# An attention kernel in which VectorE's step is reordered: the first head's maximum, the reading of outputs, the second head's maximum

## The chip, the cores and the metric
The kernel runs on one core of a Trainium2 chip. The metric is the device time of one execution in microseconds (us). Its engines work side by side and meet only at semaphores: TensorE (PE, with its weight loads as PEld), VectorE (DVE), ScalarE (ACT), GpSimd (POOL) and SyncE (SP), which issues the DMAs here.

## The reference
The input x is 2 sequences of 2048 tokens and 1024 features. A block of causal attention with 16 heads of 64 features, and then a gated low-rank layer:

```python
q = (x @ wq.T + bq).reshape(B, S, H, hd)      # k, v alike; x is the layer norm of the input
scores = jnp.einsum('bqhd,bkhd->bhqk', q, k) * inv_sqrt_hd
scores = jnp.where(causal[None, None, :, :], -jnp.inf, scores)
probs = jax.nn.softmax(scores, axis=-1)
attn = jnp.einsum('bhqk,bkhd->bqhd', probs, v).reshape(B, S, D)
return attn @ wo.T + bo
...
x = x + _layernorm(attention(_layernorm(x)))
x = x + _layernorm(ffn(_layernorm(x)))        # 8 experts, gates, the best one's low-rank update
```

## The kernel before
**Stages.** The norm of the first sequence and the first projections take some 110 us. Then come 16 pairs of heads (p = 0 to 15, eight for each sequence), about 110 us each, up to 1945 us: this is `attend_phase`. Then `finish_phase` does the output projection and the gated layer, tile by tile; the change doesn't touch it. Values of f32 are split into two f16 halves, high and low, and a product is made of three matmuls. In pairs 0 to 6 the norm of the second sequence's x runs between the other work (`norm_tiles`), in pairs 6 and 7 its transposes (`TURN_STEPS`), and in pair 15 the output weights are prepared (`center_wo`, `wo_high`, `wo_low`).

**A pair.** Its 16 rows of 128 queries are gone through in eight rounds, each of a long row (t of 8 to 15) and a short one (t of 0 to 7). A round is two steps, one round three, so a pair has NSTEP = 17 steps; a step holds eight blocks of 128 keys for each of two heads, in one or two parts. Most pairs open rounds at steps 0, 2, 4, 6, 9, 11, 13 and 15; pairs 0 and 15 take the rows upwards and open at 0, 2, 4, 6, 8, 10, 12 and 14. A part whose last block lies on the diagonal needs the causal mask in that block. Scores run LAG = 3 steps ahead of the product with v. A task is one step of one head; numbers n count tasks.

**Each engine's order is written out by hand**, one `body(p, kind)` per engine, with waits on semaphore counts. What step i of pair p does:
- TensorE (body from L613): `scores` of step i + 3 for both heads (L524), which waits until the exponential of the first head, one step before, has freed a buffer of the ring of three (`exp_done`); a unit or half a unit of the next pair's q, k or v projection (`project`, L593 to L599; `UNIT_AT` has the plan), which waits until the unit before it has been read (`full_done`); then `times_v` of step i for both heads (L547 to L549). In a step that opens a round the first head's `times_v` waits for `part_done` and `short_done`, since it overwrites the outputs of the last round.
- VectorE (body from L795): if the step opens a round, `output_read` (L746, L748, L752) and `output_sum` (L761, L764) of the last round and `row_min` (L737); then `row_max` of step i + 3 (masks L716, maxima L723, biases L728); then the low half of a weight (`split_weight`, L681 to L685), the reading of a finished unit (`unit_full`, L696, L701) and pieces of the norm.
- ScalarE (body from L946): for each head the exponentials (L894) and the high half of the probabilities (L901). Between the two heads stand `chunk_factors` (L909, which need `row_min` and the reading), once or twice a pair the high half of finished rows (`rows_high`, L919) and the high half of a unit (`unit_high`, L884).
- GpSimd (body from L1079): `long_rows` (L1062), which needs `output_sum`, the low half of the probabilities (`probs_low`, L1049) of the first head, `rows_low` (L1070), `unit_low` (L1054), and `probs_low` of the second head.
- SyncE: the DMA transposes of the probabilities (pt, L413), each after `probs_low`; finished rows are stored (L420) two steps after `rows_low`.

The lines that make VectorE's opening step before:

```python
if evacuate:
    output_read(*done)
    output_sum(*done)
if opens:
    row_min(p, r)
step = step_of(p, i, kind)
if step:
    row_max(*step)
```

Of the kernel before, what the change touches and what calls it, by code (L numbers as in the profile page):

```python
# [7 lines left out]
ALU = mybir.AluOpType  # L8
# [3 lines left out]
AX_X = mybir.AxisListType.X  # L12
# [176 lines left out]
def attend_phase(nc, x, w_pairs, mask_in, xn_scratch, o_scratch, arena, fin):  # L189
    with ExitStack() as ctx:  # L190
# [161 lines left out]
        def half_done(p):  # L352

            return first_step(p, N_ROUND // 2)
# [282 lines left out]
        def _(dve):  # L637
# [63 lines left out]
                    nc.vector.tensor_scalar(full[u % 2][:], bank, PROJ_UNSCALE,  # L701
                                            bias_cols[:, WHICH[m]:WHICH[m] + 1], ALU.mult, ALU.add).then_inc(full_done, 1)

            def row_max(p, i):
                step, n = steps_of(p)[i], NTASK * p + 2 * i
                dve.wait_ge(s_done, n + 2)
                places = []
                for part in step.parts:
                    first = places[-1][2] if places else 0
                    places.append((part, first, first + part[2] * P))  # L710
                masked = 2 * (QT * p + sum(is_diagonal(part) for step in steps_of(p)[:i] for part in step.parts))
                for h in range(2):
                    for part, first, end in places:
                        if is_diagonal(part):
                            last = s_ps[(n + h) % S_RING][:, end - P:end]
                            nc.vector.tensor_tensor(last, last, mask[:], ALU.add).then_inc(mask_done, 1)  # L716
                found = 2 * parts_before(p, i)
                for h in range(2):
                    for (t, k0, nb, acc), first, end in places:
                        if is_diagonal((t, k0, nb, acc)):  # L720
                            masked += 1
                            dve.wait_ge(mask_done, masked)
                        nc.vector.tensor_reduce(neg_max[:, step.round, acc, h:h + 1], s_ps[(n + h) % S_RING][:, first:end],  # L723
                                                AX_X, ALU.max, negate=True).then_inc(max_done, 1)
                    for (t, k0, nb, acc), first, end in places:
                        found += 1
                        dve.wait_ge(max_done, found)
                        nc.vector.tensor_scalar(exp_bias[:, step.round, acc, h:h + 1], neg_max[:, step.round, acc, h:h + 1],  # L728
                                                SOFTMAX_SCALE, LOG_P_SCALE, ALU.mult, ALU.add).then_inc(bias_done, 1)

            def row_min(p, r):

# [63 lines left out]
            def body(p, kind):  # L796
                for i in range(NSTEP):
                    r, opens = steps_of(p)[i].round, steps_of(p)[i].opens
                    done = (p, r - 1) if i else (p - 1, N_ROUND - 1)
                    evacuate = opens and done[0] >= 0  # L800
                    if evacuate:
                        output_read(*done)
                        output_sum(*done)
                    if opens:
                        row_min(p, r)
                    step = step_of(p, i, kind)
                    if step:
                        row_max(*step)
                    split = next_split(p, i - 1)
                    if split:  # L810
                        split_weight(*split)
                    for u in units_ending(kind, i):
                        unit_full(units_of(p), u)
                    for tile in norm_tiles(p, i, 0):
                        norm_stats(LN_TILES + tile, x_in[:], x_loaded[X_RING], tile)
                    for tile in norm_tiles(p, i, 1):
                        norm_apply(LN_TILES + tile, x_in[:])
                    for tile in norm_tiles(p, i, 2):
                        xn_low(LN_TILES + tile, x_in[:], xn)
                    if kind == "last":  # L820
                        if i == 6:
                            dve.wait_ge(unit_done, N_UNIT * PAIRS)
                            nc.vector.memset(fin["mix_w2"][:], 0.0).then_inc(mix_set, 1)
                            nc.vector.memset(fin["bias"][:], 0.0).then_inc(mix_set, 1)
                        if 3 <= i < 3 + WO_BY_ACT:
                            center_wo(i - 3)
                        if i in (7, 8, 9, 11):
                            center_wo({7: 4, 8: 5, 9: 6, 11: 7}[i])
                        for n, row in enumerate(("bo_row", "degen", "bias")):
                            if i == 12 + n:  # L830
                                center_rows(n, fin[row][:])
                        if 13 <= i < 13 + KT - WO_LOW_EARLY:
                            wo_low(WO_LOW_EARLY + i - 13)
                        if i == 16:
                            split_ffn_weights()
                if kind == "last":
                    output_read(p, N_ROUND - 1)
                    output_sum(p, N_ROUND - 1)
# [15 lines left out]
                unit_full(0, u)  # L854
            dve.wait_ge(consts_loaded, 32)
            for i in range(LAG):
                row_max(0, i)
                unit_full(0, LAST_CHUNK + i)
                if i == 1:
                    split_weight(1, "k")  # L860
# [3 lines left out]
        def _(act):  # L864
# [81 lines left out]
            def body(p, kind):  # L946
                for i in range(NSTEP):
                    step = step_of(p, i, kind)
                    if step:
                        exponentials(*step, 0)  # L950
                    if steps_of(p)[i].opens:
                        chunk_factors(p, steps_of(p)[i].round)
                    if i == half_done(p) or i == 0 and p > 0:
                        rows_high(2 * p + (0 if i else -1))
                    for u in units_ending(kind, i - 1):
                        unit_high(units_of(p), u)
                    if step:
                        exponentials(*step, 1)
                    if i == NSTEP - 1:
                        for u in units_ending(kind, i):  # L960
                            unit_high(units_of(p), u)
                    split = next_split(p, i)
                    if split:
                        split_weight(*split)
                    if kind == "last" and 2 <= i < 2 + WO_BY_ACT:
                        wo_sum(i - 2)
                    if kind == "last" and 6 <= i < 6 + KT:
                        wo_high(i - 6)
                    for n, row in enumerate(("bo_row", "degen", "bias")):
                        if kind == "last" and i == 11 + n:  # L970
                            row_sum(n, fin[row][:])
                    if kind == "last" and i == 15:
                        for n in range(4):
                            ffn_high(n)
                    for tile in norm_tiles(p, i, 1):
                        if tile > 0:
                            act.wait_ge(xn_stored, 16 * tile)
                        xn_high(LN_TILES + tile, x_in[:], xn)
                if kind == "last":
                    rows_high(2 * p + 1)  # L980
# [46 lines left out]
        def _(pool):  # L1027
# [50 lines left out]
            def body(p, kind):  # L1078
                for i in range(NSTEP):  # L1079
                    step = step_of(p, i, kind)  # L1080
                    if steps_of(p)[i].opens and (p or i):
                        long_rows(*((p, steps_of(p)[i].round - 1) if i else (p - 1, N_ROUND - 1)))
                    if step:
                        probs_low(*step, 0)
                    if i == half_done(p) or i == 0 and p > 0:
                        rows_low(2 * p + (0 if i else -1))
                    for u in units_ending(kind, i - 1):
                        unit_low(units_of(p), u)
                    if step:
                        probs_low(*step, 1)  # L1090
                    if i == NSTEP - 1:
                        for u in units_ending(kind, i):
                            unit_low(units_of(p), u)
                    for tile in norm_tiles(p, i, 0):
                        norm_scale(LN_TILES + tile)
                    if kind == "last" and 6 <= i < 6 + WO_LOW_EARLY:
                        wo_low(i - 6)
                if kind == "last":
                    long_rows(p, N_ROUND - 1)
                    rows_low(2 * p + 1)  # L1100
# [704 lines left out]
```

## Time and profile before

| | us |
|---|---|
| runs | 2399.49, 2399.89 (median), 2405.32 |
| profiled execution, its own time | 2399.97 |
| its span, first to last instruction | 2397.7 |
| TensorE busy | 2274.8 |
| VectorE, ScalarE, GpSimd busy | 1677.1, 1740.6, 1632.0 |
| TensorE's mean granted clock | 0.979 of full speed |

The profile is of one execution. In it an engine's time is busy, or idle with a releaser: the instruction or DMA whose semaphore ended the wait. Line numbers (L716) are those of the kernel before. Idle time under 0.15 us is not listed as a wait. An instruction may start a little before its forerunner on the same engine has ended, since they are pipelined; matmuls overlap more strongly.

### The profile page before, as it was taken

What the parts mean: (1) busy time and instruction counts of PE and PEld (TensorE: products, weight loads), DVE (VectorE), ACT (ScalarE), POOL (GpSimd) and SP (SyncE); (2) the same over time, 40 slices, a digit from 0 to 9 for tenths busy, and PEclk for the clock granted to TensorE, in tenths of its full rate; (3) what the DMA queues carried; (4) which work ended last, traced back from release to release, by engine and by line L of the source; (5) the groups of instructions that cost most, each with busy time, mean ns of one, the idle gap of its engine ahead of it and who ended that gap; (6) DMA issues with size and microseconds to landing.
All of it is one profiled execution on the core that took longest, in us unless ns stands there. A gap on an engine that the chain in (4) does not pass through costs nothing. (4 is left out here: it accounts for less than half of the span.)

```text
span 2397.7 us, 70688 instructions
## 1 busy us (share of the span) xinstructions
PE 2274.8 (95%) x28666; PEld 1450.1 (60%) x28666; DVE 1677.1 (70%) x4148; ACT 1740.6 (73%) x2380; POOL 1632.0 (68%) x1291
## 2 busy tenths in 40 slices
PE   6999999999999998899999999999999679999996
PEld 4566667575757666557575757575766445445453
DVE  8587777767777766566666666666676846777777
ACT  6577777777777766677777777777787846666665
POOL 3588888888878876778888888888898822222221
PEclk9999999999999999999999999999999789999997
DMA  9699999999999999999999999999999986656662
GB/s 246 129 196 200 197 212 203 198 193 203 213 196 202 200 202 199 206 198 194 176 197 179 190 181 182 190 183 186 181 191 198 235 166 152 170 152 171 151 166 80
DMA packets 1380627, 447.43 MB, mean 187 GB/s; under 512 B 1325104, under 2 KB 1358272, under 8 KB 1380304
## 3 DMA queue, kind: packets, MB, share of 16 engines
q1 hardware_dynamic: 1380304, 442.91, 99.4%
q8 instruction: 228, 3.74, 0.6%
q14 instruction: 95, 0.78, 0.1%
HBM read 67.95 MB, written 41.94 MB: 46 GB/s over the span
## 5 line engine op out<-in xcount | busy, mean ns | idle before, releaser
L1049 POOL TENSOR_TENSOR hl<-probs,hl 128x1024 f16<-128x1024 f32 x544 | 1166.3, 2150 | 347.6 <-ACT hl L901 345.6
L894 ACT ACTIVATE probs<-s_ps,exp_bias 128x1024 f32<-128x1024 f32 (+7 forms) x768 | 632.7, 853 | 324.4 <-DVE exp_bias L728 319.6
L723 DVE TENSOR_REDUCE neg_max<-s_ps 128x1 f32<-128x1024 f32 (+7 forms) x768 | 675.7, 904 | 166.9 <-PE s_ps L524 166.8
L901 ACT ACTIVATE hl<-probs 128x1024 f16<-128x1024 f32 x544 | 575.0, 1057 | 82.9 <-DMA pt<-hl 66.9
L547 PE MATMUL o_ps<-v,pt 128*128 128x65 f16 x4352 | 434.4, 194 | 48.7 <-DMA pt<-hl 40.7
L547 PEld LDWEIGHTS o_ps<-v,pt 128*128 128x128 f16 x4352 | 402.2, 97 | 78.5 <-DMA pt<-hl 36.4
L548 PE MATMUL o_ps<-v,pt 128*128 128x65 f16 x4352 | 434.7, 195 | 0.0
L549 PE MATMUL o_ps<-v,pt 128*128 128x65 f16 x4352 | 433.5, 193 | 0.0
L524 PE MATMUL s_ps<-nat 64*128 64x512 f16 (+3 forms) x3840 | 409.4, 351 | 22.2 <-ACT probs L894 18.8
L548 PEld LDWEIGHTS o_ps<-v,pt 128*128 128x128 f16 x4352 | 401.6, 97 | 19.2
L549 PEld LDWEIGHTS o_ps<-v,pt 128*128 128x128 f16 x4352 | 402.1, 98 | 0.0
L597 PE MATMUL u_ps<-arena,w 128*128 128x512 f16 x1000 | 380.8, 381 | 4.8 <-DVE full L696 2.8
L598 PE MATMUL u_ps<-arena,w 128*128 128x512 f16 x1000 | 379.0, 379 | 0.0
L599 PE MATMUL u_ps<-arena,w 128*128 128x512 f16 x1000 | 379.0, 379 | 0.0
L593 PE MATMUL u_ps<-w,arena 128*128 128x128 f16 x2016 | 346.1, 220 | 3.5 <-DVE arena L673 3.1
L594 PE MATMUL u_ps<-w,arena 128*128 128x128 f16 x2016 | 345.1, 220 | 0.0
L595 PE MATMUL u_ps<-w,arena 128*128 128x128 f16 x2016 | 344.9, 220 | 0.0
L524 PEld LDWEIGHTS s_ps<-nat 64*128 64x128 f16 x3840 | 164.0, 95 | 159.6 <-issue 32.3
L593 PEld LDWEIGHTS u_ps<-w,arena 128*128 128x128 f16 x2016 | 197.9, 98 | 45.0 <-issue 40.5
L701 DVE TENSOR_SCALAR full<-u_ps,bias_cols 128x512 f32<-128x512 f32 x125 | 93.8, 751 | 153.9 <-PE u_ps L599 153.6
L594 PEld LDWEIGHTS u_ps<-w,arena 128*128 128x128 f16 x2016 | 198.2, 98 | 0.1
L595 PEld LDWEIGHTS u_ps<-w,arena 128*128 128x128 f16 x2016 | 198.2, 98 | 0.0
(185 smaller groups left out, 3578.3 us busy)
## 6 DMA issues: line engine op xcount, KB each, us to landing
w_raw<-in_w_pairs SPq DMA_DIRECT2D x48, 576.0 KB, 4.8
o_scratch<-o_hl SPq DMA_DIRECT2D x64, 256.0 KB, 3.2
out<-result SPq DMA_DIRECT2D x31, 512.0 KB, 3.0
x_in<-in_x SPq DMA_DIRECT2D x27, 512.0 KB, 5.1
pt<-hl SPq DMA_TRANSPOSE x544, 5.3
xn_scratch<-xn SPq DMA_DIRECT2D x16, 512.0 KB, 4.8
xn<-in_x SPq DMA_DIRECT2D x11, 512.0 KB, 3.9
x_in_c<-in_x SPq DMA_DIRECT2D x10, 512.0 KB, 4.0
```

The costliest lines, as they stand in the source:

```text
L524: mm = nc.tensor.matmul(s_ps[(n + h) % S_RING][:, at:end], qk[HEADS[h], q, rows], qk[HEADS[h], k, keys], start=(q == q_lo), stop=(q == q_h ...
L547: nc.tensor.matmul(dst, lo, v_hi, start=first, stop=False)
L548: nc.tensor.matmul(dst, hi, v_lo, start=False, stop=False)
L549: mm = nc.tensor.matmul(dst, hi, v_hi, start=False, stop=last)
L593: nc.tensor.matmul(dst, xt[:, 1, k, toks], hi[:, k, :], start=first, stop=False)
L594: nc.tensor.matmul(dst, xt[:, 0, k, toks], lo[:, k, :], start=False, stop=False)
L595: mm = nc.tensor.matmul(dst, xt[:, 0, k, toks], hi[:, k, :], start=False, stop=last)
L597: nc.tensor.matmul(bank, lo[:, k, :], xt[:, 0, k, toks], start=first, stop=False)
L723: nc.vector.tensor_reduce(neg_max[:, step.round, acc, h:h + 1], s_ps[(n + h) % S_RING][:, first:end], AX_X, ALU.max, negate=True).then_inc ...
L894: last = nc.scalar.activation(probs_of(n)[:, cols], s_ps[n % S_RING][:, cols], ACT.Exp, bias=exp_bias[:, step.round, acc, h:h + 1], scale= ...
L901: nc.scalar.activation(hl_of(n, 0), probs_of(n), ACT.Copy).then_inc(p_hi_done, 1)
L1049: nc.gpsimd.tensor_tensor(hl_of(n, 1), probs_of(n), hl_of(n, 0), ALU.subtract).then_inc(p_lo_done, 1)
```

## The change
VectorE's `row_max` now does one head per call. In a step it does the first head (masks, maxima, biases), then `output_read`, `row_min`, the second head, and `output_sum` last. So in every step the second head's masks come after the first head's biases, and in an opening step the reading comes after the first head. ScalarE does `rows_high` after the second head's exponentials instead of before `unit_high`. GpSimd does `long_rows` after the first head's `probs_low` and `unit_low`, and `rows_low` after the second head's `probs_low`. TensorE, SyncE, all tiles and all instructions stay as they are.

```diff
@@ VectorE
-            def row_max(p, i):
+            def row_max(p, i, h):
                 step, n = steps_of(p)[i], NTASK * p + 2 * i
                 dve.wait_ge(s_done, n + 2)
...
-                masked = 2 * (QT * p + sum(is_diagonal(part) for step in steps_of(p)[:i] for part in step.parts))
-                for h in range(2):
-                    for part, first, end in places:
-                        if is_diagonal(part):
-                            last = s_ps[(n + h) % S_RING][:, end - P:end]
-                            nc.vector.tensor_tensor(last, last, mask[:], ALU.add).then_inc(mask_done, 1)
-                found = 2 * parts_before(p, i)
-                for h in range(2):
-                    for (t, k0, nb, acc), first, end in places:
...
+                diagonals = sum(is_diagonal(part) for part in step.parts)
+                masked = 2 * (QT * p + sum(is_diagonal(part) for step in steps_of(p)[:i] for part in step.parts)) + h * diagonals
+                found = 2 * parts_before(p, i) + h * len(step.parts)
+                for part, first, end in places:
+                    if is_diagonal(part):
+                        last = s_ps[(n + h) % S_RING][:, end - P:end]
+                        nc.vector.tensor_tensor(last, last, mask[:], ALU.add).then_inc(mask_done, 1)
+                for (t, k0, nb, acc), first, end in places:
...
                     evacuate = opens and done[0] >= 0
+                    step = step_of(p, i, kind)
+                    if step:
+                        row_max(*step, 0)
                     if evacuate:
                         output_read(*done)
-                        output_sum(*done)
                     if opens:
                         row_min(p, r)
-                    step = step_of(p, i, kind)
                     if step:
-                        row_max(*step)
+                        row_max(*step, 1)
+                    if evacuate:
+                        output_sum(*done)
@@ ScalarE
-                    if i == half_done(p) or i == 0 and p > 0:
-                        rows_high(2 * p + (0 if i else -1))
                     for u in units_ending(kind, i - 1):
                         unit_high(units_of(p), u)
                     if step:
                         exponentials(*step, 1)
+                    if i == half_done(p) or i == 0 and p > 0:
+                        rows_high(2 * p + (0 if i else -1))
@@ GpSimd
+                    if step:
+                        probs_low(*step, 0)
+                    for u in units_ending(kind, i - 1):
+                        unit_low(units_of(p), u)
                     if steps_of(p)[i].opens and (p or i):
                         long_rows(*((p, steps_of(p)[i].round - 1) if i else (p - 1, N_ROUND - 1)))
                     if step:
-                        probs_low(*step, 0)
+                        probs_low(*step, 1)
                     if i == half_done(p) or i == 0 and p > 0:
                         rows_low(2 * p + (0 if i else -1))
-                    for u in units_ending(kind, i - 1):
-                        unit_low(units_of(p), u)
-                    if step:
-                        probs_low(*step, 1)
```

## Rows read from the trace of the kernel before

**Rows 1.** The page, part 1: busy us of each engine, share of span, instructions.

```profile
PE 2274.8 (95%) x28666; PEld 1450.1 (60%) x28666; DVE 1677.1 (70%) x4148; ACT 1740.6 (73%) x2380; POOL 1632.0 (68%) x1291
```

**Rows 2.** Waits of TensorE, whole span: total us, times, longest us.

```profile
PE o_ps L547 <- DMA pt<-hl: 40.7, 31, 3.2
PE s_ps L524 <- ACT probs L894: 18.8, 23, 2.5
...
PE o_ps L547 <- DVE o_rows L752: 6.4, 3, 3.1
```

**Rows 3.** Stretches: length, busy us of five engines, granted clock, DMA share, GB/s.

```profile
480.00:540.00 60.00, 56.84 (x942) 43.06 (x942) 41.09 (x96) 44.70 (x58) 48.24 (x30) 0.97 1.18 193
600.00:660.00 60.00, 57.90 (x977) 44.54 (x974) 43.37 (x110) 44.88 (x59) 50.09 (x33) 1.00 1.16 215
...
1080.00:1740.00 660.00, 659.73 (x9596) 444.00 (x9592) 445.31 (x1137) 512.80 (x674) 538.26 (x328) 1.00 1.07 186
```

**Rows 4.** Waits of TensorE, 170 to 1860 us.

```profile
PE s_ps L524 <- ACT probs L894: 12.7, 16, 2.5
```

**Rows 5.** Waits of TensorE, 1860 to 1945 us.

```profile
PE o_ps L547 <- DMA pt<-hl: 19.9, 17, 2.9
```

**Rows 6.** Timeline of VectorE, pair 10, step 9: start us, us, instruction, idle before.

```profile
1340.91 0.43 DVE L746 TENSOR_TENSOR o_part<-o_ps,factor 128x260 f32<-128x260 f32 x1 [0.76 <-PE o_ps L549]
...
1341.45 0.29 DVE L752 TENSOR_TENSOR o_rows<-o_ps,inv_short 128x128 f32<-128x128 f32 x1
1341.66 0.41 DVE L761 TENSOR_REDUCE o_long<-o_part 128x130 f32<-128x260 f32 x1
...
1342.19 0.16 DVE L737 TENSOR_REDUCE bias_min<-exp_bias 128x2 f32<-128x4 f32 x1
1342.33 0.89 DVE L716 TENSOR_TENSOR s_ps<-s_ps,mask 128x128 f32<-128x128 f32 x4
1343.13 1.27 DVE L723 TENSOR_REDUCE neg_max<-s_ps 128x1 f32<-128x384 f32 x2
1344.32 0.27 DVE L728 TENSOR_SCALAR exp_bias<-neg_max 128x1 f32<-128x1 f32 x2
```

**Rows 7.** Timeline of TensorE, pair 10, steps 2, 4 and 9.

```profile
1294.02 1.48 PE L524 MATMUL s_ps<-nat 64*128 64x512 f16 x18
...
1300.62 0.19 PE L547 MATMUL o_ps<-v,pt 128*128 128x65 f16 x1
...
1307.72 1.47 PE L524 MATMUL s_ps<-nat 64*128 64x512 f16 x12
...
1311.72 0.19 PE L547 MATMUL o_ps<-v,pt 128*128 128x65 f16 x1
...
1340.81 1.48 PE L524 MATMUL s_ps<-nat 64*128 64x384 f16 x18
...
1344.91 0.19 PE L547 MATMUL o_ps<-v,pt 128*128 128x65 f16 x1
```

**Rows 8.** Timeline of both engines, pair 15, step 8.

```profile
1885.57 0.29 DVE L752 TENSOR_TENSOR o_rows<-o_ps,inv_short 128x128 f32<-128x128 f32 x1
...
1886.01 0.19 PE L547 MATMUL o_ps<-v,pt 128*128 128x65 f16 x1 [2.12 <-DVE o_rows L752]
```

**Rows 9.** Timeline of VectorE and TensorE, pair 4 into pair 5.

```profile
675.00 3.15 DVE L667 SCALAR_TENSOR_TENSOR xn<-x_in,xn 128x1024 f16<-128x1024 f32 x1
678.07 1.21 DVE L723 TENSOR_REDUCE neg_max<-s_ps 128x1 f32<-128x1024 f32 x1
...
680.76 0.39 PE L524 MATMUL s_ps<-nat 64*128 64x512 f16 x2 [0.95 <-ACT probs L894]
```

**Rows 10.** Timeline of VectorE, ScalarE and TensorE, pair 4, steps 9 and 10.

```profile
629.69 0.41 DVE L746 TENSOR_TENSOR o_part<-o_ps,factor 128x260 f32<-128x260 f32 x1
...
633.32 1.26 ACT L894 ACTIVATE probs<-s_ps,exp_bias 128x384 f32<-128x384 f32 x2 [5.36 <-DVE exp_bias L728]
...
634.73 0.39 PE L524 MATMUL s_ps<-nat 64*128 64x512 f16 x2 [0.63 <-ACT probs L894]
```

More of the change, by code:

```diff
@@ L717, in row_max @@
-                found = 2 * parts_before(p, i)
-                for h in range(2):
-                    for (t, k0, nb, acc), first, end in places:
[L720 to L729, printed above, removed]
+                diagonals = sum(is_diagonal(part) for part in step.parts)
@@ new lines, in row_max @@
+                masked = 2 * (QT * p + sum(is_diagonal(part) for step in steps_of(p)[:i] for part in step.parts)) + h * diagonals
[5 more added lines that the diff above has]
+                for (t, k0, nb, acc), first, end in places:
+                    if is_diagonal((t, k0, nb, acc)):
+                        masked += 1
+                        dve.wait_ge(mask_done, masked)
+                    nc.vector.tensor_reduce(neg_max[:, step.round, acc, h:h + 1], s_ps[(n + h) % S_RING][:, first:end],
+                                            AX_X, ALU.max, negate=True).then_inc(max_done, 1)
@@ L731, in row_min @@
+                for (t, k0, nb, acc), first, end in places:
+                    found += 1
+                    dve.wait_ge(max_done, found)
+                    nc.vector.tensor_scalar(exp_bias[:, step.round, acc, h:h + 1], neg_max[:, step.round, acc, h:h + 1],
+                                            SOFTMAX_SCALE, LOG_P_SCALE, ALU.mult, ALU.add).then_inc(bias_done, 1)
             def row_min(p, r):
@@ L856, in _ @@
             for i in range(LAG):
-                row_max(0, i)
+                for h in range(2):
+                    row_max(0, i, h)
                 unit_full(0, LAST_CHUNK + i)
```

## The prediction

> **What bounds the kernel now.** I read the busy shares first. TensorE is busy for 95% of the span and no other engine for more than 73% [rows 1], so the first question is what TensorE waits for. Its waits answer that [rows 2]: 40.7 us for transposed probabilities (pt) to land, 18.8 us for an exponential that frees a score buffer, and 6.4 us, in three places, for VectorE's reading of outputs. Then I asked where these lie. From 1080 to 1740 us, pairs 8 to 13 of the 16, TensorE is busy 659.73 of 660 us at full clock, the other three engines under 82% [rows 3]. There the schedule hides everything beside TensorE: a new order on the other engines can gain nothing in these six pairs, it can only uncover something. What can be gained lies in pairs 0 to 7 and in the last pair: of the waits for an exponential, 12.7 us in 16 places lie between 170 and 1860 us [rows 4]. The last pair (1860 to 1945 us) has 19.9 us of waits for pt [rows 5].
>
> **The step that the change touches.** A pair has 17 steps, eight of which open a round. In an opening step TensorE issues the scores of three steps ahead, then a piece of projection, then times_v, whose first matmul must wait until VectorE has read the last round's outputs. Times from the scores' end (S), in pair 10, step 9: the scores run from 1340.81 to 1342.29, times_v starts at 1344.91, which is S + 2.62 [rows 7]. VectorE reads from 1340.91 to 1341.74, sums, takes the minimum and starts the masks at 1342.33, 0.04 us after S [rows 6]. So today reading, sum and minimum (1.42 us from 1340.91 to 1342.33) fit under the 1.48 us of scores and cost nothing. The maxima aren't held up by them either. This is the profile's point against the change: the first head's maximum can't start before S whatever the order is, and the reading loses its cover.
>
> **VectorE's new step, priced from the same rows.** First head: masks at S + 0.04, two instead of four. Four masks put the maximum 0.80 later, so 0.20 each [rows 6]; with two the maximum starts at about S + 0.43. Maxima and biases of one head take 1.46 (1343.13 to the end of the biases at 1344.59) and end at S + 1.90. The next instruction starts about 0.08 before its forerunner's end (o_long at 1341.66, o_rows ends at 1341.74), so the reading starts at S + 1.82 and ends 0.83 later at S + 2.65. From VectorE's end to TensorE's first matmul is 0.15 (1885.86 to 1886.01) [rows 8]. So times_v may start at S + 2.80.
>
> It is due at S + 2.62 after half a v unit, at S + 2.53 after half a q or k unit (1309.19 to 1311.72), and at S + 5.1 after a whole unit (1295.50 to 1300.62) [rows 7]. Whole units hide the reading; half units miss it by 0.18 or 0.27. With one diagonal block (one mask) the reading ends 0.11 earlier, miss 0.16; with none it is in time. Pairs 1 to 5 and 8 to 13 have the half-unit openings 4, 9, 13 and 15 (0.16 + 0.18 + 0.18 + 0.27 = 0.79 us a pair). Over pairs 0 to 14 there are 18 of 0.27, 29 of 0.18 and 9 of 0.16: 11.5 us. Some 1.2 us of it fall in pair 7 and late in pair 14, where TensorE waits for pt anyway: **10.3 us**. The unknown is the fit of a few tenths: 0.15 less at each of 56 places is 8 us less, 0.1 more is 6 us more.
>
> **What comes behind it in the step.** Reading, minimum, the second head (masks at S + 2.7, biases done at S + 4.6), then sum and reciprocal end at about S + 5.1, where the second head's bias ended at S + 3.7 before. In openings 4 and 13 a unit's result is read after that (0.7 us) and TensorE wants its bank at the next projection, due at about S + 5.6: it misses by about 0.1. GpSimd's finished row (0.4 us) now waits behind the first head's subtraction (2.13 us) and a unit, and in opening 9 ScalarE's copy of finished rows, now last, waits for it before the next step's first exponential: 0.05 to 0.1. Together 0.3 us in each of 11 pairs: **3 us**.
> VectorE is 1.4 us later at the end of an on-time opening step. Where it then has splits or norm work and no idle time before the next maximum, and ScalarE and TensorE have no slack either, TensorE pays that. Pair 4, step 15 is the pattern: xn for 3.15 us to 678.15, the maximum at 678.07, and TensorE 0.95 us late at 680.76 [rows 9]. Five openings are like this (pair 0 step 2, pair 1 steps 6 and 15, pairs 4 and 5 step 15), with 0.7 to 1.4 us left after the slack of each: **5 us**. Elsewhere ScalarE and TensorE have more slack than the delay.
>
> **What it gives.** The first head's exponential starts 0.4 us earlier where VectorE was on time with two diagonals, but pairs 8 to 13 have no wait for it. It gains where VectorE was late. Pair 4, step 9: reading at 629.69 instead of 628.5, ScalarE idle 5.36 us until 633.32, TensorE 0.63 late at 634.73 [rows 10]. Masks first would start that exponential 1.4 us earlier; this stall and the next one, of 0.46 at 640.90, go. With smaller ones: **minus 1.6 us**. In step 4 of pairs 1 and 5 VectorE is late too: stalls of 1.70 and 1.16 us for the exponential go, but the reading, put behind the maximum, makes times_v wait 1.65 and 1.11: nothing.
> In the last pair the openings 6 to 12 have no projection and times_v would wait up to 7.5 us in all for the reading (four times S + 2.8 against its start now). But the second head's pt mostly lands later anyway [rows 5], and its stalls take the delay: **1 us**, with bounds 0 and 7.5. The row copies that move on GpSimd and ScalarE cost nothing more there: both heads' subtractions now precede them. That moves transposes earlier, up to 4 us of the 19.9 if TensorE gets them sooner.
> SyncE's queue doesn't change in order; the stores of rows are issued two steps after the copy, so 3 us of delay are covered.
>
> **Sum:** 10.3 + 3 + 5 - 1.6 + 1 = 17.7 us on the span of 2397.7 [rows 1, 3] gives 2415.4. The profiled execution took 2399.97 us, 2.3 more than its span and 0.1 above the median of the runs shown, so the forecast is **2418 us**.
>
> **The rivals.**
> *Hidden after all* (2396 to 2407): the new waits are 0.16 to 0.27 us each and rest on handoffs read from a late place [rows 8]. If they are 0.15 shorter and the slack behind takes the rest, about 5 us stay: 2405. For it: all margins are small. Against: four independent rows put the reading behind S + 2.53.
> *Faster* (2387): in pairs 0 to 7 and the last, where VectorE or ScalarE are late, the earlier first head takes away the waits for exponentials. All 12.7 us of [rows 4] gone and nothing else uncovered gives 2385.0 and 2387. It decides from the point where more of these stalls hang on VectorE's order than on ScalarE's own load. For it: pair 4, step 9. Against: most of the others follow a split, a norm copy or a row copy on ScalarE, which the change moves by less than a step.
> *VectorE's backlog* (2436): norm work and splits in pairs 0 to 6 push the maxima over more steps than the five counted. Twice the 5 us, the last pair's 7.5 in full and the upper end of the 56 waits (6 more) give 18 us more.
> *The clock* (2445): stalls of up to 1.2 us left the granted clock at 1.00 from 600 to 660 us; in the window from 480 to 540 us with one wait of 3.2 us it was 0.97, which is 1.8 us lost [rows 3, 2]. If the new short waits brought one such drop in each of 15 pairs, 27 us would come on top of the forecast. The Trainium skill, "TensorE: Matmul & The Clock Gate", "A second HAM failure mode: psum-queue depth-cycling", has a kernel whose frequent tiny idles between groups of matmuls made the clock swing and cost throughput; by that rule the clock would be this rival, and the trace of before doesn't bear it out for waits this short.
>
> **How the numbers follow.** Forecast 0.50 (its own range 2407 to 2430), hidden 0.24, faster 0.14, backlog 0.08, clock 0.04. The range for 8 in 10 reaches from 2394, which leaves out most of the faster case, to 2438, which takes in half of the backlog case; the clock is left out. Faster and slower begin 0.3% from before, 7.2 us, about what a measurement of this kernel can tell from no change: above 2407.1 lie the forecast, the backlog and the clock, 0.62; within lies 0.24; below 2392.7 lies 0.14.
>
> **What would show it.** In the profile after, TensorE's waits should have a new entry for o_rows in pairs 8 to 13, some 24 waits of 0.1 to 0.3 us (those under 0.15 us are not listed, but TensorE's busy time from 1080 to 1740 us falls below 659.7), at half-unit openings alone. VectorE should idle up to S in opening steps instead of before the reading. The wait for the exponential at step 10 of pair 4 should be gone and the one at the turn into pair 5 be longer. If TensorE has no new waits in pairs 8 to 13, the handoff is mis-sized; if the waits for pt in pair 7 or the last pair shrink by over 5 us, the transposes were not the limit there.

## The result and the profile after

| | before | after |
|---|---|---|
| median of the runs, us | 2400.76 | 2440.76 |
| lowest and highest | 2399.49, 2405.32 | 2435.84, 2444.03 |
| ratio, 95% interval | | 1.0159 [1.0146, 1.0172] |
| profiled execution: its own time, span | 2399.97, 2397.7 | 2441.16, 2439.0 |

The change makes the kernel 40 us slower. The forecast was 2418 us with a range up to 2438: the sign was right, the size less than half of it.

The page, part 1, and the waits of TensorE over the whole span (us in total, times, longest), of after:

```profile
PE 2285.1 (94%) x28666; PEld 1448.3 (59%) x28666; DVE 1725.1 (71%) x4148; ACT 1746.8 (72%) x2380; POOL 1659.1 (68%) x1291
...
PE s_ps L524 <- ACT probs L897: 40.8, 32, 2.7
PE o_ps L547 <- DMA pt<-hl: 28.5, 26, 3.3
PE o_ps L547 <- DVE o_rows L751: 17.6, 11, 4.8
```

Against [rows 1, 2] VectorE is busy for 48 us more and GpSimd for 27 us more, although both execute the same instructions as often. That is the first thing to see: some instructions have become longer. TensorE's waits for the exponential have grown from 18.8 to 40.8 us; those for the reading from 6.4 to 17.6, most of it in the last pair, where those for pt fell.

The stretches of [rows 3] that are comparable (length, busy us of PE, PEld, DVE, ACT, POOL, granted clock, DMA share, GB/s), and TensorE's waits from 1110 to 1770 us, of after:

```profile
1080.00:1740.00 660.00, 645.88 (x9261) 430.33 (x9257) 453.19 (x1095) 502.14 (x658) 533.44 (x318) 1.00 1.04 181
...
PE s_ps L524 <- ACT probs L897: 9.7, 11, 1.3
PE o_ps L547 <- DVE o_rows L751: 0.6, 2, 0.4
```

In this stretch TensorE is idle for 14.1 us where it was idle for 0.3 in [rows 3], at a clock of 1.00. The listed waits are mainly for exponentials, up to 1.3 us long, and the forecast has no such term there.

Since TensorE's order is the same in both kernels, its step ends can be subtracted one by one (after minus before, from the two traces). In pairs 9, 10, 11 and 13, the ordinary pairs of what follows, the difference is 3.1 us each (in pair 12 it is 3.5, with 0.44 at step 14):

| step | us a pair | what TensorE waits for |
|---|---|---|
| 4, 9, 13, 15 | 0.18, 0.21, 0.21, 0.30 | the reading of outputs, as forecast (0.16, 0.18, 0.18, 0.27) |
| 5, 14, 11 | 0.02, 0.08, 0.10 | the unit's result, and the rows on ScalarE (forecast 0.3 together) |
| 8 | 0.59 | exponential, not forecast |
| 0 of the next pair | 1.40 | exponential, not forecast |

The forecast's terms for such a pair were 0.79 and 0.3, and 1.11 was measured. The other 2.0 us are new. Over all pairs the turns (step 0 of pairs 2 to 14) make 21.3 us and step 8 (pairs 1 to 14) 7.8 us of the span's 41.3.

**What happens before the turn.** Timeline of VectorE, then of GpSimd, then of TensorE, after, from pair 10, step 15 into pair 11 (start us, us, instruction, idle before):

```profile
1416.65 1.57 DVE L681 TENSOR_SCALAR bv_row<-w_raw 128x128 f32<-128x128 f32 x1
1418.14 2.19 DVE L685 SCALAR_TENSOR_TENSOR w<-w_raw,w 128x1024 f16<-128x1024 f32 x1
1420.26 1.21 DVE L722 TENSOR_REDUCE neg_max<-s_ps 128x1 f32<-128x1024 f32 x1
...
1416.01 2.13 POOL L1052 TENSOR_TENSOR hl<-probs,hl 128x1024 f16<-128x1024 f32 x1 [3.54 <-ACT hl L904]
1418.10 1.15 POOL L1057 TENSOR_TENSOR nat<-full,nat 128x512 f16<-128x512 f32 x1
1419.22 1.37 POOL L1065 TENSOR_TENSOR o_rows<-o_long,inv_long 128x128 f32<-128x128 f32 x1
...
1422.95 1.26 PE L524 MATMUL s_ps<-nat 64*128 64x512 f16 x14 [1.32 <-ACT probs L897]
```

The same place before, VectorE and then GpSimd:

```profile
1385.03 0.22 DVE L681 TENSOR_SCALAR bv_row<-w_raw 128x128 f32<-128x128 f32 x1
1385.16 1.22 DVE L685 SCALAR_TENSOR_TENSOR w<-w_raw,w 128x1024 f16<-128x1024 f32 x1
1387.01 1.23 DVE L723 TENSOR_REDUCE neg_max<-s_ps 128x1 f32<-128x1024 f32 x1 [0.63 <-PE s_ps L524]
...
1382.37 0.39 POOL L1062 TENSOR_TENSOR o_rows<-o_long,inv_long 128x128 f32<-128x128 f32 x1
1386.19 2.17 POOL L1049 TENSOR_TENSOR hl<-probs,hl 128x1024 f16<-128x1024 f32 x1 [3.43 <-ACT hl L901]
```

Before, the bias row took 0.22 us and the weight split 1.22, with GpSimd idle until 1386.19, and 0.63 us were left before the next maximum. After, the bias row starts at 1416.65, while GpSimd's subtraction runs, and ends at 1418.22, just after that ends (1418.14). The split then stands against GpSimd's unit, which ends at 1419.25, and ends at 1420.33: 1.08 us later, nearly its own 1.22. And GpSimd's row product, 0.39 us when alone, starts at 1419.22 and ends at 1420.59, when the split is over. They don't slow each other in proportion: whichever comes second stands still until the first has ended. Bias row and split end 2.3 us later than their own lengths ask for (1416.65 + 1.35 = 1418.00). The next maximum starts 2.8 us after the end of its scores (1417.49) instead of at once, its exponential is late too, and TensorE starts the scores 1.32 us late.

The other place is the split of k's weight in step 6, timeline of VectorE and GpSimd, after:

```profile
1356.03 2.84 DVE L685 SCALAR_TENSOR_TENSOR w<-w_raw,w 128x1024 f16<-128x1024 f32 x1
...
1355.65 2.13 POOL L1052 TENSOR_TENSOR hl<-probs,hl 128x1024 f16<-128x1024 f32 x1 [2.48 <-ACT hl L904]
1357.74 2.14 POOL L1057 TENSOR_TENSOR nat<-full,nat 128x512 f16<-128x512 f32 x1
```

The split again ends (1358.87) 1.09 us after the subtraction (1357.78). Two steps on, at 1362.09, TensorE waits 0.52 us for an exponential.

**How often.** By line, min/median/max in ns; first before (L681, L685), then after (L681, L685):

```profile
L681 DVE TENSOR_SCALAR bv_row<-w_raw x16: 216/218/227, 13.6 to 1725.0; 128x128 f32<-128x128 f32 x16
L685 DVE SCALAR_TENSOR_TENSOR w<-w_raw,w x48: 1212/1216/2344, 13.7 to 1752.4; 128x1024 f16<-128x1024 f32 x48
```

```profile
L681 DVE TENSOR_SCALAR bv_row<-w_raw x16: 217/1575/1633, 13.4 to 1766.2; 128x128 f32<-128x128 f32 x16
L685 DVE SCALAR_TENSOR_TENSOR w<-w_raw,w x48: 1212/2190/2839, 13.6 to 1794.0; 128x1024 f16<-128x1024 f32 x48
```

The two meet because of when each starts. VectorE reaches the bias row at S + 5.0 where it was S + 3.6, and GpSimd's first subtraction of the step starts at about S + 4.4 (S + 4.8 before). Before, the split was through, or had at least begun; now the subtraction gets in first. The Trainium skill, "SBUF — State Buffer", "Who interferes with whom", states this rule: an instruction of VectorE with two inputs in SBUF, or a tensor_scalar in a 2-port mode, and a GpSimd instruction that reads SBUF exclude each other for a whole instruction, and the order of issue decides who blocks. The rows agree in both directions. The split has two inputs in SBUF; the bias row is a tensor_scalar with one, and that it ran in a 2-port mode no run shows by itself, only that it was held up like the split.

### The profile page after: what moved, and what is told of

It is laid out like the page before. It is cut to its first block and busy times, and to the rows that moved or that the text cites. A ratio compares the mean times of both kernels' runs of the same rounds, so it can differ in the third digit from the quotient of the medians.

```text
span 2439.0 us, 70688 instructions
## 1 busy us (share of the span) xinstructions
PE 2285.1 (94%) x28666; PEld 1448.3 (59%) x28666; DVE 1725.1 (71%) x4148; ACT 1746.8 (72%) x2380; POOL 1659.1 (68%) x1291
## 5 line engine op out<-in xcount | busy, mean ns | idle before, releaser
L524 PE MATMUL s_ps<-nat 64*128 64x512 f16 (+3 forms) x3840 | 410.2, 352 | 45.0 <-ACT probs L897 40.8
L717 DVE TENSOR_TENSOR s_ps<-s_ps,mask 128x128 f32<-128x128 f32 x512 | 128.7, 291 | 214.6 <-PE s_ps L524 214.3
L593 PEld LDWEIGHTS u_ps<-w,arena 128*128 128x128 f16 x2016 | 197.4, 98 | 45.0 <-issue 40.6
L597 PEld LDWEIGHTS u_ps<-arena,w 128*128 128x128 f16 x1000 | 97.8, 98 | 169.9 <-issue 69.3
L594 PEld LDWEIGHTS u_ps<-w,arena 128*128 128x128 f16 x2016 | 197.7, 98 | 0.1
```

What stands on the lines that cost most here:

```text
L524: mm = nc.tensor.matmul(s_ps[(n + h) % S_RING][:, at:end], qk[HEADS[h], q, rows], qk[HEADS[h], k, keys], start=(q == q_lo), stop=(q == q_h ...
L593: nc.tensor.matmul(dst, xt[:, 1, k, toks], hi[:, k, :], start=first, stop=False)
L594: nc.tensor.matmul(dst, xt[:, 0, k, toks], lo[:, k, :], start=False, stop=False)
L597: nc.tensor.matmul(bank, lo[:, k, :], xt[:, 0, k, toks], start=first, stop=False)
```

## The experiments

Ten kernels, all compared with the kernel before on the same chip (there 2400.89, 2401.99 and 2405.76 us in the three groups of runs). "As before" and "as after" name the order of one engine's instructions in an opening step. The cuts of code that show an order are shortened: conditions and arguments are partly left out. "Less than after" compares the two medians; the kernels before beside them differ by 1.2 us at most.

**1. VectorE's change alone.** VectorE as after; ScalarE and GpSimd as before:

```diff
 # ScalarE, GpSimd: the bodies of the kernel before
 # VectorE:
+row_max(*step, 0); output_read(*done); row_min(p, r)
+row_max(*step, 1); output_sum(*done)
```

> The change on VectorE alone; ScalarE and GpSimd keep the order of before. Theory (the loss is VectorE's: the reading behind the first head's maximum, and a weight split that runs while GpSimd subtracts): nearly the whole loss stays, 2430 to 2440 us, TensorE busy from 1080 to 1740 us stays near 646 us. Rival (the loss comes from finished rows on GpSimd and ScalarE being late): 2400 to 2412 us and busy over 656 us.

Measured 2414.48 us, ratio 1.0056 [1.0036, 1.0075]: 13.6 us of the 40, so the expectation was wrong. The ordinary pair loses 1.5 us: the same waits for the reading, 0.49 at step 11, nothing at the turn, nothing at step 8. The timeline (VectorE, GpSimd, pair 10, step 15) says why:

```profile
1395.36 0.21 DVE L681 TENSOR_SCALAR bv_row<-w_raw 128x128 f32<-128x128 f32 x1
1395.48 1.22 DVE L685 SCALAR_TENSOR_TENSOR w<-w_raw,w 128x1024 f16<-128x1024 f32 x1
...
1395.52 1.43 POOL L1065 TENSOR_TENSOR o_rows<-o_long,inv_long 128x128 f32<-128x128 f32 x1 [4.24 <-DVE inv_long L763]
```

VectorE is as late as in after. But GpSimd starts its step with the row product, which waits for the inverse that VectorE writes just ahead of the split. So the split is always first and GpSimd stands still (1.43 us instead of 0.39), which costs TensorE nothing.

**2. The rows alone.** VectorE as before; ScalarE and GpSimd as after (the second and third parts of the change's diff).

> The change on ScalarE and GpSimd alone; VectorE keeps the order of before. Theory: 2398 to 2405 us, no new wait of TensorE in pairs 8 to 13. Rival (rows late are the loss): over 2420 us.

Measured 2406.59, ratio 1.0027 [1.0017, 1.0037], a little above the range expected, and the expectation of no new wait in pairs 8 to 13 was wrong: it loses 0.70 us at step 11 of each of them and nothing else in an ordinary pair. ScalarE, pair 10:

```profile
1360.17 1.06 ACT L919 ACTIVATE o_hl<-o_rows 128x1024 f16<-128x1024 f32 x1 [0.59 <-POOL o_rows L1062]
1361.14 1.10 ACT L894 ACTIVATE probs<-s_ps,exp_bias 128x1024 f32<-128x1024 f32 x1
```

GpSimd's row is late, ScalarE's copy waits 0.59 us for it, and the next step's exponential stands behind. Together the parts cost 13.6 + 5.7 = 19 us. The whole costs 40: half of the loss is an interaction. That 19 us is near the 17.7 forecast for the whole is in part luck: the 0.49 and 0.70 us at step 11 were forecast as 0.1 at most.

**3. The reading put first again.** After, with VectorE's reading ahead of the first head (then minimum, second head, sum):

```diff
-row_max(*step, 0); output_read(*done)
+output_read(*done); row_max(*step, 0)
```

> The kernel after, with the reading of outputs put back ahead of the first head's maximum; row_min, the second head and the sum stay as changed. Theory: the half-unit openings lose their 0.2 to 0.3 us waits (1.1 us a pair), but the split after the sum stays late by about 0.8 us instead of 1.4 and still meets GpSimd's subtraction: 2405 to 2420 us. Rival (the reading's place is the whole loss): within 4 us of before, 2397 to 2405 us.

Measured 2404.56, ratio 1.0013 [1.0001, 1.0025], which fits the range of the rival and lies just below that of the theory. All waits for the reading in pairs 8 to 13 are gone and 0.31 us at step 11 are left. VectorE, GpSimd, pair 10, step 15:

```profile
1386.23 0.21 DVE L681 TENSOR_SCALAR bv_row<-w_raw 128x128 f32<-128x128 f32 x1
1386.35 1.22 DVE L685 SCALAR_TENSOR_TENSOR w<-w_raw,w 128x1024 f16<-128x1024 f32 x1
...
1386.35 3.21 POOL L1052 TENSOR_TENSOR hl<-probs,hl 128x1024 f16<-128x1024 f32 x1 [3.47 <-ACT hl L904]
```

The bias row now starts at S + 4.3, only 0.12 us before the subtraction. VectorE keeps its 0.21 and 1.22 us, and it is GpSimd that takes 3.21 us instead of 2.13: the theory had the meeting right and who would stand still wrong. Moving the reading by one place brings back both the four short waits and the order of the two engines; by itself this run can't say which of them is worth what.

**4. Two splits one step earlier.** After, with the splits of k and v moved ahead by one step:

```diff
-SPLITS = {"mid": {2: "q", 5: "k", 14: "v"}, ...
+SPLITS = {"mid": {2: "q", 4: "k", 13: "v"}, ...
```

> The kernel after, with the k and v weight splits of ordinary pairs moved by a step, so that VectorE's part follows steps 5 and 14, which open no round, instead of 6 and 15. Theory: the stalls of 1.4 us at the turn of the pair and 0.6 us at step 8 vanish in 11 pairs: about 20 us faster than after, 2412 to 2424 us, with the 1.1 us a pair of late readings left. Rival (the turn's stall is the reading's delay alone): no change from after, 2436 to 2444 us.

Measured 2449.09, ratio 1.0200 [1.0182, 1.0219]: a miss of 25 us. The stalls at the turn and at step 8 are gone in pairs 8 to 13 (0.00 against before), but a new one of 1.7 to 7.6 us stands at step 6 of 11 pairs, 43 us in all. ScalarE waits for the DMA of the raw weights 88.0 us in all, against 20.8 in after: with two steps instead of three between the splits of q and k, k's weight is asked for before it has been loaded, and VectorE waits behind ScalarE. So the experiment removed the suspected cost and added another one.

```profile
ACT w L877 <- DMA w_raw<-in_w_pairs: 88.0, 16, 9.9
...
DVE bias_cols L683 <- ACT w L877: 60.0, 15, 7.2
```

**5. Only v's split one step earlier.**

```diff
-SPLITS = {"mid": {2: "q", 5: "k", 14: "v"}, ...
+SPLITS = {"mid": {2: "q", 5: "k", 13: "v"}, ...
```

> The changed kernel with one weight split of an ordinary pair moved one step ahead, that of v from behind step 15 (an opening step) to behind step 14. Theory (this split at this place is what makes the turn into the next pair late): the turn's stall, 1.32 us at step 0 of the next pair, goes in the 11 pairs concerned, the 0.5 us at step 8 stay, as do the waits for the outputs: 13 to 16 us faster than the changed kernel, 2424 to 2429. Rival (the turn is late by the sum and the reading, which stand behind the first head's maximum, and not by the split): 2436 to 2442.

Measured 2417.59, ratio 1.0065 [1.0050, 1.0080]: 23 us less than after. The 1.40 us at the turn are gone in each of pairs 9 to 13, the 3.3 and 3.9 us at the turns into pairs 5 and 6 as well, and the 0.59 us at step 8 remain. Over all pairs the turns give 20.7 us back. It was better than expected because I had counted 11 turns at 1.4 and not the two larger ones; some 2.5 us more are a start of pair 0 that came earlier in this trace.

**6. GpSimd as before**, VectorE and ScalarE as after:

```diff
+if steps_of(p)[i].opens and (p or i): long_rows(...)
 if step: probs_low(*step, 0)
+if i == half_done(p) or i == 0 and p > 0: rows_low(...)
 for u in units_ending(kind, i - 1): unit_low(units_of(p), u)
-if steps_of(p)[i].opens and (p or i): long_rows(...)
 if step: probs_low(*step, 1)
-if i == half_done(p) or i == 0 and p > 0: rows_low(...)
```

> VectorE and ScalarE in the order of the changed kernel, GpSimd in the order of the kernel before. Theory (VectorE's weight split is held up by GpSimd's subtraction, 2.13 us long, which in the changed kernel starts just ahead of it): here GpSimd begins an opening step with the rows' product, which waits for the inverse that VectorE writes right ahead of the split, so the split starts first and keeps its 1.2 us; the stalls at the turn (1.4 us) and at step 8 (0.6 us) of each pair are gone, and what is left is VectorE's order alone (2414) and up to 0.7 us in each of 11 pairs at step 11 (8 us): 2414 to 2425, with TensorE busy near 651 to 654 us between 1080 and 1740. Rival (the opening steps are late because ScalarE's rows come last, GpSimd's order is of no account): 2433 to 2442, as the changed kernel.

Measured 2408.85, ratio 1.0029 [1.0018, 1.0040], 5 us below the range expected. VectorE's lateness is untouched (the bias row starts at S + 5.0), and 32 us of the loss are gone with the order of one other engine. VectorE, GpSimd, pair 10, step 15:

```profile
1389.59 0.21 DVE L681 TENSOR_SCALAR bv_row<-w_raw 128x128 f32<-128x128 f32 x1
1389.71 1.21 DVE L685 SCALAR_TENSOR_TENSOR w<-w_raw,w 128x1024 f16<-128x1024 f32 x1
...
1389.75 1.43 POOL L1065 TENSOR_TENSOR o_rows<-o_long,inv_long 128x128 f32<-128x128 f32 x1 [4.25 <-DVE inv_long L763]
```

Step 11 gains 0.11 us where experiment 1 lost 0.49 and up to 0.7 was expected: with the row product early, ScalarE's copy is better off last.

**7. The same lateness without a second operand in SBUF.** After, with the split's two instructions on VectorE replaced, from the weights of pair 2 on, by sums of the same lengths that read one operand. The low halves of the weights and the biases are left out from there on.

```diff
+if p >= 2:
+    nc.vector.tensor_reduce(split_to[:, 0:1], w_raw[:, KT * P:W_COLS], AX_X, ALU.add)
+    nc.vector.tensor_reduce(split_to[:, 1:2], w_raw[:, 0:KT * P], AX_X, ALU.add).then_inc(w_lo_done, 1)
+    return
```

> The changed kernel, but from the third pair on VectorE's two instructions of a weight split (the bias and the low half) are sums over a row of the same lengths that read one operand in SBUF and write one number; the low halves of the weights and the biases are not computed for those pairs. Theory (the split is slow because VectorE and GpSimd then share the way to SBUF, and the split with two operands there is the one that must wait): it takes about 1.2 us again wherever it stands, the stall at the turn goes and that at step 8 too, about 2.0 us in each of some 10 pairs: 2415 to 2424. If only the writing or any reading in SBUF is enough to be held up, it stays at 2433 to 2442. Rival (the split comes 1.3 us later than before, and that lateness alone makes the next scores' maximum late): 2433 to 2442 as well, but with the split at 1.2 us in the trace.

Measured 2411.74, ratio 1.0042 [1.0027, 1.0057], 29 us less than after and 3 below the range expected. Every order, GpSimd's included, is that of after. VectorE, GpSimd, pair 10, step 15:

```profile
1396.06 0.27 DVE L682 TENSOR_REDUCE split_to<-w_raw 128x1 f32<-128x128 f32 x1
1396.24 1.21 DVE L683 TENSOR_REDUCE split_to<-w_raw 128x1 f32<-128x1024 f32 x1
1397.37 1.21 DVE L727 TENSOR_REDUCE neg_max<-s_ps 128x1 f32<-128x1024 f32 x1
...
1395.42 2.14 POOL L1057 TENSOR_TENSOR hl<-probs,hl 128x1024 f16<-128x1024 f32 x1 [3.53 <-ACT hl L909]
1397.51 1.16 POOL L1062 TENSOR_TENSOR nat<-full,nat 128x512 f16<-128x512 f32 x1
1398.62 0.40 POOL L1070 TENSOR_TENSOR o_rows<-o_long,inv_long 128x128 f32<-128x128 f32 x1
```

The instructions lie beside GpSimd's subtraction as in after, and neither side is held up. Both unforecast stalls are 0.00 in pairs 8 to 13, and an ordinary pair loses 1.11 us: the terms of the forecast, no more. This settles that the exclusion is the cause and lateness alone is not. For the split it doesn't tell whether the second operand or the wide output in SBUF matters, since the sums lack both. For the bias row it tells that a second operand isn't needed: the row reads one operand and took 1.57 us beside the subtraction in after, and the sum over the same 128 columns, which writes one number instead of 128, takes 0.27.

**8. Masks given out by head, nothing else.** VectorE: reading, sum, minimum, then first head, then second; the rest as before:

```diff
-row_max(*step)
+row_max(*step, 0)
+row_max(*step, 1)
```

> The kernel before with one thing changed: mask, maximum and bias are given out head by head; both still stand behind the reading and the sum, and ScalarE and GpSimd keep their order. Theory (the loss needs the reading of the outputs behind the first head, and the split behind the sum): the reading ends where it did, so no half-unit opening is late; where a step has a diagonal block, the first exponential may start up to 0.2 us sooner, which TensorE does not wait for: 2397 to 2403, ratio 0.9985 to 1.001. Rival (giving the masks out by head costs VectorE a wait for each mask's end, which the backlog of the opening steps can't hide): 2404 to 2412.

Measured 2398.84, ratio 0.9990 [0.9980, 0.9999]. TensorE is busy for 660.00 of 660 us between 1080 and 1740. The part of the change that starts the first exponential earlier costs nothing and gains 0.1 us in each of the saturated pairs.

**9 and 10. Can both kernels be beaten?** Experiment 8 with ScalarE as after; and reading, first head, minimum, second head, sum with ScalarE as after and GpSimd as before:

```
9:  output_read; output_sum; row_min; row_max(*step, 0); row_max(*step, 1)
10: output_read; row_max(*step, 0); row_min; row_max(*step, 1); output_sum
```

> The kernel before with masks, maximum and bias given out head by head (behind reading and sum), and ScalarE's copy of finished rows last in its step; GpSimd as before. Theory (the 0.7 us at step 11 that the late rows cost come from GpSimd's product being late, which ScalarE's copy and then its next exponential wait for): with GpSimd's order of before the copy finds its rows ready, step 11 costs nothing, and the time is that of masks by head alone: 2395 to 2402, at best 0.2% faster than before. Rival (ScalarE's order alone makes step 11 late by 0.7 us): 2404 to 2410.

> VectorE reads the outputs first, then first head, minimum, second head, sum; ScalarE in the order of the changed kernel, GpSimd in that of the kernel before. Theory (what was left of the loss with the reading put first, 0.31 us at step 11 of each pair, comes from GpSimd's late product): it goes, and the earlier first exponential gains a few of the waits in pairs 1 to 7: 2395 to 2402. Rival (the sum behind the second head is what makes step 11 and the last pair late): 2403 to 2409.

Measured 2402.26, ratio 0.9986 [0.9977, 0.9995], and 2401.43, ratio 0.9984 [0.9975, 0.9993] (before took 2405.76 on this chip). Step 11 costs nothing in either, which confirms that the 0.70 of experiment 2 hangs on GpSimd's late product. Both are 0.15% faster than the kernel before and 1.7% faster than the changed one; between these two and experiment 8 no difference can be measured. In each of the saturated pairs they gain 0.1 us, some 0.5 us in all. Where the other 3 to 4 us of the medians come from the traces don't show: against the trace of before, pairs 1 to 7 together are 1.5 us (experiment 9) and 0.4 us (experiment 10) slower, so a gain this small stays unexplained.

## Why the prediction was wrong in size

**What bounds it.** Right. TensorE was saturated, and the change could only uncover something there.

**The new step's arithmetic.** Right. Against [rows 6, 7], VectorE and the start of `times_v` after, pair 10, step 9 (scores from 1370.74 to S = 1371.88):

```profile
1371.93 0.50 DVE L717 TENSOR_TENSOR s_ps<-s_ps,mask 128x128 f32<-128x128 f32 x2 [2.17 <-PE s_ps L524]
1372.33 1.28 DVE L722 TENSOR_REDUCE neg_max<-s_ps 128x1 f32<-128x384 f32 x2
1373.53 0.27 DVE L727 TENSOR_SCALAR exp_bias<-neg_max 128x1 f32<-128x1 f32 x2
1373.75 0.43 DVE L745 TENSOR_TENSOR o_part<-o_ps,factor 128x260 f32<-128x260 f32 x1
...
1374.29 0.29 DVE L751 TENSOR_TENSOR o_rows<-o_ps,inv_short 128x128 f32<-128x128 f32 x1
...
1376.36 0.43 DVE L760 TENSOR_REDUCE o_long<-o_part 128x130 f32<-128x260 f32 x1
1376.82 0.17 DVE L763 RECIPROCAL inv_long<-o_long 128x2 f32<-128x2 f32 x1
...
1374.73 0.19 PE L547 MATMUL o_ps<-v,pt 128*128 128x65 f16 x1
```

The reading starts at S + 1.87 and ends at S + 2.70 (forecast 1.82 and 2.65), `times_v` starts at S + 2.85 (2.80), and sum and reciprocal end at S + 5.11 (5.1). VectorE idles up to S, as was said. An ordinary pair's four waits are 0.90 us (forecast 0.79), so the term of 10.3 us was sound; by the same factor (0.90 to 0.79) it comes to some 12.

**The unit's result and the rows (3 us).** 0.20 us measured in an ordinary pair against 0.3: right in size.

**The backlog (5 us), and the sentence "Elsewhere ScalarE and TensorE have more slack than the delay".** This is the step that failed. It counted a delay of 1.4 us as 1.4 us. The delayed instruction, though, runs at its old length only if nobody else holds what it needs, and at S + 5 GpSimd does. In pair 10, step 15, the split ends at S + 8.7 where it ended at S + 5.0: the delay of 1.4 became 3.7 us, and the next maximum starts 2.8 us after the end of its scores. In experiment 7, with the delay of 1.4 alone, it starts 0.5 us after (1397.37 against 1396.90), and TensorE loses nothing there. So the slack was there as said for 1.4 us; it doesn't cover 3.7, and the turns gave 21.3 us and step 8 gave 7.8. Experiments 5, 6 and 7 take 23, 32 and 29 us of the loss away, each by another handle.

Without the exclusion (experiment 7) the turns into pairs 2 and 5 are 0.5 and 0.7 us faster than before, and the turn into pair 6 and step 8 of pair 1 are 0.5 us slower each, so in these four of the five backlog openings little of the 5 us is there. The fifth, pair 0, step 2, makes step 4 3.1 us late in after, and in experiment 7 as well. That is no exception: pair 0 splits the weights of pair 1, which experiment 7 leaves as they are. VectorE there, in experiment 7:

```profile
125.25 1.63 DVE L686 TENSOR_SCALAR bv_row<-w_raw 128x128 f32<-128x128 f32 x1
126.80 2.19 DVE L690 SCALAR_TENSOR_TENSOR w<-w_raw,w 128x1024 f16<-128x1024 f32 x1
```

With GpSimd as before (experiment 6) they take 0.21 and 1.22 us and step 4 is 0.7 us late, which is the size forecast for one such opening; the other 2.4 are the exclusion. Turns, step 8 and this place together put its price at about 30 of the 41.3 us.

**It could have been read from the trace of before.** [rows 9] has xn at 3.15 us, and I took that for its length. Its line, before, min/median/max in ns, and GpSimd beside it:

```profile
L667 DVE SCALAR_TENSOR_TENSOR xn<-x_in,xn x16: 1212/1788/3152, 148.6 to 867.5; 128x1024 f16<-128x1024 f32 x16
...
674.89 2.17 POOL L1049 TENSOR_TENSOR hl<-probs,hl 128x1024 f16<-128x1024 f32 x1 [2.47 <-ACT hl L901]
677.03 2.13 POOL L1054 TENSOR_TENSOR nat<-full,nat 128x512 f16<-128x512 f32 x1
```

The same instruction takes 1.21 us or 3.15, and in the second case it ends 1.09 us after GpSimd's subtraction (677.06 to 678.15), while GpSimd's unit next takes 2.13 instead of 1.16. And the margin could be read: before, the split started at 1385.16 and the subtraction at 1386.19, 1.0 us apart. A bias row and a split that come 1.4 us later, and a subtraction that comes 0.4 us earlier with its exponential, turn that order round. The change also took away, on GpSimd, the wait for `inv_long` that had kept the order whatever the delay; I costed that move at the row's 0.4 us alone.

**The gains (minus 1.6 us).** At pair 4, steps 7 and 10, TensorE is 0.53 and 0.70 us earlier and 0.32 at step 11, so 1.55 us as forecast. Not forecast: pair 3, step 10, where before waited 3.2 us for pt, is 3.9 us shorter, with 1.0 us given back one step later. That step is 0.4 to 3.9 us shorter in the traces of all ten experiments too, so how much of it is the change's is open. In pairs 1 and 5, step 4 costs 1.54 and 1.00 us (the reading) and the next step gains 1.75 and 1.22: near nothing, as said.

**The last pair (1 us).** Pair 15's steps differ by up to 3 us in both signs and sum to 1.4 us. The waits for the reading rose from 6.4 to 14.0 us there ([rows 2]: all of before's lay in this pair) and those for pt fell from 19.9 to 12.5 [rows 5]: the stalls took the delay, as said. By the prediction's own sign (pt waits shrinking by over 5 us) the transposes were then not the only limit there; the reading took their place and the sum of both stayed at 26 us.

**The rivals.** *The clock* is out: the mean is 0.981 against 0.979 and 1.00 in pairs 8 to 13, with waits of 0.2 to 1.4 us in every pair. (The prediction misread one row: from 600 to 660 us the waits of before are 0.6 us at most; its wait of 1.2 us lies between 680 and 720, in a stretch whose clock is 1.00 too.) The rule of the Trainium skill that the prediction named beside it ("TensorE: Matmul & The Clock Gate", "A second HAM failure mode: psum-queue depth-cycling") isn't borne out for waits of this kind. *Hidden after all* and *Faster* fall with the ordinary pair: its waits are there in full, and the stalls that went (3.9 and 1.6 us in pairs 3 and 4) are few. *VectorE's backlog* named the right engine, but priced norm work and not the exclusion, and by 2436 it ended short: that it lies within 5 us of the measured time is luck. Some 1 to 4 us are probably no part of the change: the first step of pair 0 ends 3.7 us later in after's trace, 2.7 of them gathered before its first scores, and between 1.0 and 3.9 later in those of the experiments, with no relation to their time.

## What to carry to other kernels

An instruction that is moved keeps its length only if its new place has the same neighbours on the other engines: look at the min and max of its line, and where they differ by as much as an instruction of another engine takes, find that engine and the order in which the two start. Where two engines exclude each other, a wait that seems to cost something may be what keeps them in the cheap order (here GpSimd's wait for the inverse). Measure parts of a change together too: 14 and 6 us alone made 40.

## What the runs showed of the hardware

VectorE and GpSimd do not meet only at semaphores, as the start of this document has it. Some of their instructions exclude each other as wholes, in either direction: the bias row (128x128) 0.22 us alone and 1.57 behind the subtraction; the split (128x1024, two operands in SBUF) 1.22 alone and up to 2.84; GpSimd's row product 0.39 and 1.43, its unit 1.16 and 2.14, its subtraction 2.13 and 3.21. In each case the second ends about its own length, less 0.1 us, after the first. Maxima that read PSUM (1.17 to 1.23 us in all 320 over 1024 columns of after), and sums over one operand in SBUF (0.27 and 1.21 us), kept their lengths beside GpSimd. In the ordinary pairs TensorE lost nothing at the turn and at step 8 where GpSimd was second (experiments 1, 3 and 6) and lost time where VectorE was second by 1.6 us or more, since the next maximum stands behind the split, while GpSimd has idle time after its step. A bias row held up by 0.45 us (0.67 instead of 0.22, experiments 4 and 5) cost nothing.
